# Thirteen tiles prepared in the opening of an attention layer, and the row maxima sent to the rows of q through memory

## What is computed

```python
xn = layernorm(x)
# attention: 16 heads of q, 8 of k and v (two q heads share one k and v), 16 wide
energy = einsum('nqhd,nkhd->nhqk', q, k) + alibi          # -|i-j| * 2**-(head+1)
attn = softmax(energy / sqrt(16))
att = einsum('nhqk,nkhd->nqhd', attn, v).reshape(n, s, 256) @ Wo.T + bo
# linear with quantised rows
x_scale = max(amax(abs(xn)), 1e-6) / 127
lin = (clip(round(xn / x_scale), -128, 127) @ weight_q.T) * x_scale * weight_scale + bias
out = x + att + lin
```

## Time and profile before

| | us |
|---|---|
| median of 3 runs | 1567.06 |
| the profiled execution, whole | 1568.38 |
| its span in the trace | 1566.4 |
| busy: TensorE / VectorE / ScalarE / GpSimd | 1497.0 / 1394.6 / 1184.8 / 1076.1 |

### The profile page before, as it was taken

The page is one execution under the profiler, slowest core; times in us unless marked ns, Lnnn a source line. Parts: engine busy times, 40 slices in busy tenths (PEclk is TensorE's granted clock), DMA queues, the critical chain, the costliest instruction groups (busy, mean ns, idle before and its releaser), DMA issues.

```text
span 1566.4 us, 42517 instructions
## 1 busy us (share of the span) xinstructions
PE 1497.0 (96%) x16284; PEld 583.0 (37%) x16284; DVE 1394.6 (89%) x1698; ACT 1184.8 (76%) x2331; POOL 1076.1 (69%) x1627
## 2 busy tenths in 40 slices
PE   5899999999999999999989999999999999999998
PEld 5333333333333333333333334333333333333333
DVE  5999989999899998999979999899998988999981
ACT  3467777777787776887767887777877777788885
POOL 5467777777788876787757877677877776533332
PEclk9999999999999999999999999999999999999999
DMA  6522243333334334333333433433333332312212
GB/s 169 140 76 71 74 100 81 93 98 81 105 83 108 96 79 109 91 92 101 84 92 94 105 85 91 103 98 96 97 83 96 94 92 65 82 49 68 72 44 62
DMA packets 197291, 140.98 MB, mean 90 GB/s; under 512 B 107040, under 2 KB 165728, under 8 KB 197088
## 3 DMA queue, kind: packets, MB, share of 16 engines
q1 hardware_dynamic: 197088, 138.27, 34.2%
HBM read 81.40 MB, written 35.63 MB: 75 GB/s over the span
## 4 chain that ended last, share of the span: by engine, by line
PE 47%; DVE 30%; SPq 9%; issue 8%; DMA 3%; POOL 2%; ACT 0%; POOLq 0%; DVEq 0%; ACTq 0%
DVE row_max L999 27%; PE ps_ring L1279 15%; PE ps_pv L1355 13%; PE ps_row L1296 9%; PE ps_ring L1395 4%; PE ps_ring L1415 3%; SPq L464 2%; SPq L468 2%; SPq L506 2%; DMA q<-neg_max_t 1%; SPq L472 1%; PE ps_ring L1398 1%; DMA k<-k_alibi 1%; DVE pv_turned L1039 1%; PE ps_ring L1409 1%
## 5 line engine op out<-in xcount | busy, mean ns | idle before, releaser
L999 DVE TENSOR_REDUCE row_max<-ps_row 128x1 f32<-128x1024 f32 x1024 | 1199.5, 1213 | 114.7 <-PE ps_row L1298 99.4
L1171 ACT ACTIVATE probs<-ps_ring 128x512 f32<-128x512 f32 x2048 | 1084.5, 601 | 245.2 <-PE ps_ring L1279 242.6
L1279 PE MATMUL ps_ring<-q,k 122*32 122x512 bf16 x8192 | 636.6, 383 | 19.9 <-DMA q<-neg_max_t 19.0
L762 POOL TENSOR_TENSOR probs<-probs,near 128x256 f32<-128x256 f32 x512 | 375.2, 733 | 324.8 <-ACT probs L1171 318.9
L1355 PE MATMUL ps_pv<-probs,v_unit 128*32 128x512 f32 x4096 | 533.5, 596 | 0.0
L1279 PEld LDWEIGHTS ps_ring<-q,k 122*32 122x32 bf16 x8192 | 215.1, 95 | 518.0 <-ACT probs L1171 324.7
L1296 PE MATMUL ps_row<-k,q 64*128 64x512 bf16 x944 | 326.2, 385 | 25.8 <-DVE row_max L999 11.4
L1298 PE MATMUL ps_row<-k_again,q_again 64*128 64x512 bf16 x944 | 326.0, 385 | 0.0
L1296 PEld LDWEIGHTS ps_row<-k,q 64*128 64x128 bf16 x944 | 84.2, 93 | 320.3 <-issue 199.6
L1355 PEld LDWEIGHTS ps_pv<-probs,v_unit 128*32 128x32 f32 x4096 | 124.7, 110 | 54.2 <-issue 7.7
L1298 PEld LDWEIGHTS ps_row<-k_again,q_again 64*128 64x128 bf16 x944 | 84.0, 92 | 0.0
(11 more groups left out here) (84 smaller groups left out, 1012.0 us busy)
## 6 DMA issues: line engine op xcount, KB each, us to landing
parts_dram<-parts SPq DMA_DIRECT2D x59, 288.0 KB, 3.0
q_again<-q SPq DMA_DIRECT2D x63, 256.0 KB, 3.3
token_b<-token_dram SPq DMA_DIRECT2D x53, 256.0 KB, 4.1
q<-parts_dram SPq DMA_DIRECT2D x128, 96.0 KB
k<-parts_dram SPq DMA_DIRECT2D x256, 32.0 KB
q<-parts_dram SPq DMA_DIRECT2D x128, 64.0 KB
att_dram<-att_unit SPq DMA_DIRECT2D x126, 64.0 KB
att_t<-att_dram SPq DMA_DIRECT2D x56, 128.0 KB, 2.9
```

Source lines behind the costliest of these rows:

```text
L762: pool.tensor_tensor(here, here, near[:, u % KV_HEADS, :].rearrange("p (e n) -> p e n", e=GROUP), ALU.mult).then_inc(weighted, 1)
L999: dve.tensor_reduce(row_max[:, par, e, qb:qb + 1], ps_row[qb % 2][:, :], AX_X, ALU.max, negate=True).then_inc(row_max_found, 1)
L1171: act.activation(probs[:, c % PBUFS, e, h * HALF:(h + 1) * HALF], ring_bank(u, c, e, h), ACT.Exp, scale=SCALE).then_inc(ring_freed, 1)
L1279: mm = pe.matmul(to[at, :], weights[:, at], moving, start=start, stop=stop)
```

## The change

Three things. **(1)** PREP_AHEAD goes from 11 to 13. The opening makes 13 tiles, tiles made in units come one pair earlier relative to their batch (tile 15 in unit 3), and late_set with all its branches goes: every set is loaded by next_set at the start of its unit, and every row block in the units is a half_row_block. In the opening the store of tile 8 goes ahead of the first set, the stores of the others behind set 1; the first rounding step of tiles 0 to 7 goes from GpSimd to VectorE (round_first), in place. In units 0 and 1 the normalising and statistics of the two tiles are spread over blocks 1 and 3. out_tile takes the place of near_bias. **(2)** place_max, four transfers inside SBUF, becomes store_max (neg_max_t to max_dram, one transfer) and place_max (max_dram to the two rows of q, one transfer, which waits for the store). **(3)** In SP's unit the order behind load_token is new: store_max(u+1), in even units store_att(u-1), load_again(u+3), place_max(u+1), load_att_t, store_out.

```diff
-PREP_AHEAD = 11
+PREP_AHEAD = 13
-OTHERS_BEHIND = [1 + 22 * k // 12 for k in range(PREP_AHEAD + 2)]
+OTHERS_BEHIND = [1 + 22 * k // (PREP_AHEAD + 1) for k in range(PREP_AHEAD + 2)]
-def late_set(u):
-
-    return u >= SETS - 1 and last_tile(u) >= PREP_AHEAD and made_unit(last_tile(u)) == u - SETS + 1
...
+            def store_max(u):
+
+                sp.wait_ge(max_turned, u + 1)
+                sp.dma_start(max_dram[u % PAIR, :, :].rearrange("x (j r) -> j x r", r=TURN),
+                             neg_max_t[:, :]).then_inc(max_stored, 16)
+
             def place_max(u, slot):
 
-                sp.wait_ge(max_turned, u + 1)
-                for j in range(P // TURN):
-                    sp.dma_start(q_set[SET_K:COL_K, slot, :, :].rearrange(
-                        "m e (a j r) -> m (e a) j r", j=P // TURN, r=TURN)[:, :, j, :],
-                        neg_max_t[j * TURN:(j + 1) * TURN, :]).then_inc(set_loaded[slot], 16)
+                sp.wait_ge(max_stored, 16 * (u + 1))
+                sp.dma_start(q_set[SET_K:COL_K, slot, :, :].rearrange("m e n -> m (e n)"),
+                             max_dram[u % PAIR, :, :].rearrange("(m x) n -> m (x n)", m=MAX_ROWS)).then_inc(
+                                 set_loaded[slot], 16)
...
-            for t in range(BLOCKS):
+            for t in range(BLOCKS + 1):
                 store_parts(t, t % 2)
-            wait_parts(BLOCKS, 0)
+            wait_parts(0)
             load_set(0, 0)
-            for t in range(BLOCKS, PREP_AHEAD):
-                store_parts(t, t % 2)
             sp.dma_start(near_bias[:, :, :], diag.rearrange("g p n -> p g n")).then_inc(
                 near_loaded, 16)
             load_set(1, 1)
+            for t in range(BLOCKS + 1, PREP_AHEAD):
+                store_parts(t, t % 2)
...
             store_token(PREP_AHEAD)
+            store_max(0)
+            load_again(2, 2)
             place_max(0, 0)
-            load_again(2, 2)
...
-                if u + 2 < UNITS and late_set(u + 2):
-                    load_again(u + 2, (u + 2) % SETS)
-                if f["row_set"] and not late_set(u + 3):
+                if f["row_set"]:
                     next_set(u + 3)
...
                 if not f["last"]:
-                    place_max(u + 1, (u + 1) % SETS)
+                    store_max(u + 1)
                 if f["prev"] and u % PAIR == 0:
                     store_att(u - 1)
+                if f["row_set"]:
+                    load_again(u + 3, (u + 3) % SETS)
+                if not f["last"]:
+                    place_max(u + 1, (u + 1) % SETS)
                 for t in f["next_att"]:
                     load_att_t(t, t % 2)
-                if f["row_set"]:
-                    if late_set(u + 3):
-                        next_set(u + 3)
-                    else:
-                        load_again(u + 3, (u + 3) % SETS)
...
+            def round_first(t):
+                dve.wait_ge(first_scale_ready, 2)
+                dve.wait_ge(xn_turned, t + 1)
+                dve.tensor_scalar(xn_of(t), xn_of(t), token_of(t)[:, XINV:XINV + 1], ROUND,
+                                  ALU.mult, ALU.add).then_inc(first_rounded, 1)
...
                 dve.wait_ge(max_split, 2 * (u + 1))
                 if u > 0:
-                    slot = (u - 1) % SETS
-                    dve.wait_ge(set_loaded[slot], set_count(u - 1, slot, WHOLE_SET))
+                    dve.wait_ge(max_stored, 16 * u)
...
-                        if not late_set(u + 2):
-                            wait_again(u + 2)
-                    if late_set(u + 2):
-                        row_block(u + 2, (u + 2) % SETS, 0, i - BLOCKS)
-                    else:
-                        half_row_block(u + 2, (u + 2) % SETS, 0, i - BLOCKS)
+                        wait_again(u + 2)
+                    half_row_block(u + 2, (u + 2) % SETS, 0, i - BLOCKS)
```

More of the change, by code:

```diff
@@ L125, in flags_of @@
         factor=[PREP_AHEAD + 2] * (u == 0) + [u + PREP_AHEAD + 3] * (u + PREP_AHEAD + 3 < TILES),
-        first_linear=([u // 2] if u < 18 else [9, 10] if u == 18 else []) if not pairs else [],
+        first_linear=([u // 2] if u < 18 else [9, 10] if u == 18 else
+                      list(range(11, PREP_AHEAD)) if u == 20 else []) if not pairs else [],
         xt=u + 2 + PREP_AHEAD < TILES,
@@ L157 @@
 SET_LOADS = K_LOADS + GROUP * Q_LOADS + ALIBI_LOADS
-WHOLE_SET = SET_LOADS + P // TURN
+WHOLE_SET = SET_LOADS + 1
 def alibi_rows():
@@ L190, in build @@
 def build(nc, x, x_t, wqk_t, wv_t, wo_t, wo_last_t, w8_t, w_scale, bias_attn, bias_lin, q_alibi, k_alibi, diag,
-          eye, parts_dram, token_dram, att_dram, out):
+          eye, parts_dram, token_dram, att_dram, max_dram, out):
     ctx = ExitStack()
@@ L256, in build @@
         att_last = sb("att_last", [P, EC, SEQ])
-        out_tile = sb("out_tile", [P, 2, EMBED])
+        out_tile = near_bias[:, :, :].rearrange("p g n -> p (g n)").bitcast(F32)[:, 0:2 * EMBED].rearrange(
+            "p (b n) -> p b n", n=EMBED)
         ps_row = [ctx.enter_context(nc.psum_tensor(f"ps_row{i}", [P, SEQ], F32)) for i in range(2)]
@@ L316, in build @@
         first_rows_loaded = sem("first_rows_loaded")
-        first_parts_stored = [sem(f"first_parts_stored{i}") for i in range(FIRST_PARTS)]
+        first_parts_stored = [sem(f"first_parts_stored{t}") for t in range(PREP_AHEAD)]
         first_amax_ready = sem("first_amax_ready")
         first_scale_ready = sem("first_scale_ready")
+        first_rounded = sem("first_rounded")
         first_lin_ready = sem("first_lin_ready")
@@ L356, in build @@
         max_turned = sem("max_turned")
+        max_stored = sem("max_stored")
         ring_filled = sem("ring_filled")
@@ L417, in wait_stored @@
         def wait_stored(eng, t):
+            if t < FIRST_PARTS:
+                return
             if t < PREP_AHEAD:
-                wait(eng, first_parts_stored[t % FIRST_PARTS], 16 * (t // FIRST_PARTS))
+                eng.wait_ge(first_parts_stored[t - FIRST_PARTS], 16)
             elif t < PREP_AHEAD + 2:
-                i = t % 2
-                eng.wait_ge(first_parts_stored[i], 16 * len(range(i, PREP_AHEAD, FIRST_PARTS)))
+                last = max(k for k in range(PREP_AHEAD) if k % FIRST_PARTS == t % 2)
+                eng.wait_ge(first_parts_stored[last], 16)
             else:
@@ L442, in store_parts, with wait_parts @@
                     parts_of(t).rearrange("p m (c n) -> p (m c) n", n=P)).then_inc(stored, 16)
[L444 to L448, removed]
+            def wait_parts(u):
+                last = last_tile(u)
+                for t in range(last + 1 - BLOCKS, min(last + 1, PREP_AHEAD)):
+                    sp.wait_ge(first_parts_stored[t], 16)
                 for t in (PREP_AHEAD, PREP_AHEAD + 1):
-                    wait(sp, parts_stored[t % 2], 16 * len(range(t, tiles, 2)))
+                    wait(sp, parts_stored[t % 2], 16 * len(range(t, last + 1, 2)))
             def load_set(u, slot):
@@ L709, in quantise @@
             def quantise(t):
[L711 to L715, removed]
+                if t >= BLOCKS:
+                    pool.wait_ge(first_scale_ready, 4)
+                    pool.wait_ge(xn_turned, t + 1)
+                    pool.tensor_scalar(xn_of(t), xn_of(t), token_of(t)[:, XINV:XINV + 1], ROUND,
+                                       ALU.mult, ALU.add).then_inc(first_rounded, 1)
+                pool.wait_ge(first_rounded, t + 1)
                 wait(pool, xq_turned, t - 1)
-                pool.tensor_scalar(xq[:, t % 2, :], xround[:, :], -ROUND, Q_MAX, ALU.add,
+                pool.tensor_scalar(xq[:, t % 2, :], xn_of(t), -ROUND, Q_MAX, ALU.add,
                                    ALU.min).then_inc(xq_ready, 1)
@@ L990, in _ @@
                     find_first_scales(0, BLOCKS, 0)
+                for k in range(max(0, PAIR * (t - BLOCKS + 1)), min(BLOCKS, PAIR * (t - BLOCKS + 2))):
+                    round_first(k)
             find_first_scales(BLOCKS, PREP_AHEAD, 2)
@@ L1069, in unit, with here @@
                 at_sums, at_norm = (5, BLOCKS) if apart else (3, 3)
+                made = 1 if u < PAIR else PAIR
+                def here(c):
+                    return slice(0, made) if c == 1 else slice(made, PAIR)
                 for c in range(BLOCKS):
@@ L1085, in unit @@
                             turn_back(u - 1)
-                    if c == 1:
-                        for t in f["normed"]:
+                    if c in (1, 3):
+                        for t in f["normed"][here(c)]:
                             normalise(t, t % 2)
@@ L1090, in unit @@
                             find_scale(t, t % 2)
-                        for t in f["stats"]:
+                        for t in f["stats"][here(c)]:
                             wait(dve, x_loaded, 16 * (t - X_AHEAD + 1))
@@ L1210, in _ @@
             for i in range(2, FIRST_PARTS):
```

(3 more changed lines are left out.)

10 lines of the change are left out of this document (6 added, 4 removed).

## The result

The changed kernel takes 1716.64 us in the median (1714.80 to 1718.91); the kernel before, run beside it, 1570.11. The ratio is 1.0932 (95% interval 1.0887 to 1.0976). 1709 was predicted. The profiled execution has a span of 1713.0 us, 146.6 more than before.

The account below looks back on a forecast made before the run. TensorE, busy 1497.0 of 1566.4 us, was taken to bound the kernel. 1566.4 + 111 + 37 + 22 - 27 - 3.9 + 3 = 1708.5 of span, so 1709 against 1567.06; range 1645 to 1759.

Parts of the forecast that it names:

- The main step: In 30 even units SP issues the load behind store_att and load_again, so the next unit starts 3.7 us late: +111.
- The bound "behind q_again": Upper bound for the load's landing in even units, queued behind q_again's 3.3 us: next unit 4.3 us late.
- the row of the 128 KB load: Profile row of a load from memory, 2.5 us issue to landing, taken as the time of the load of the maxima.
- The clock: Lower TensorE clock after 27 of the 30 waits, 1.39 us each: +37 (21 to 42).
- The odd units' waits: In 25 odd units store (3.5) plus load (2.5) land 0.9 us late for the next unit: +22 (0 to 47).
- Its 1672 for the sum: Total in us if each transfer leg took the skill page's 2.0 us; the odd units' wait would vanish.
- The gain: No late sets at the 7 batch boundaries, -27, and two tiles less among the units, -3.9.
- The opening: Unit 0 starts later through the store and load of its maxima and two more tiles: +3 (0 to 5).
- The first: Rival: load of the maxima not late in even units, no waits or slow clocks, 1539 us; chance 0.07.
- The second: Rival: even-unit waits come, but the clock stays up and odd units arrive in time, 1637 to 1650; chance 0.13.
- The third: Rival: store and load each take 4.5 us, even units 5.7 late, about 1799 us; chance 0.05.
- The fourth: Rival: wait and gain cancel, needing a delay of 1 us in 30 units; chance 0.01.

Follow-up runs that it names:

- experiment 3: Changed kernel with its 13 tiles in the opening, but the four transfers inside SBUF and SP's order of the kernel before; 1541.16 us, ratio 0.9826.
- experiment 7: Changed kernel with load_again issued behind the load of the maxima, store_att still ahead of it; 1626.47 us, ratio 1.0354.
- experiment 1: Changed kernel with store_att in even units issued behind the load of the maxima instead of ahead of it; 1561.62 us, ratio 0.9957.
- experiment 5: Changed kernel, SP's order untouched, with VectorE's turn of the output in even units after row block 9 instead of 13; 1565.22 us, ratio 0.9969.
- experiment 4: Kernel before (11 tiles, late sets) with the maxima by one store and one load, store_att behind the load; 1610.97 us, ratio 1.0271.
- experiment 8: Kernel of experiment 3 with the opening's 512 KB load of wo_last moved behind load_token; 1538.45 us, ratio 0.9796 to the kernel before.
- experiment 9: Changed kernel with SP's order store_max, place_max, store_att, load_again, the load of the maxima directly behind its store; 1547.65 us, ratio 0.9846.
- experiment 2: Kernel before with its four transfers inside SBUF moved behind store_att and load_again in SP's order; 1789.88 us, ratio 1.1411.
- experiment 6: Changed kernel with 48 useless matmuls run by TensorE in each odd unit from 3 on before it waits for the maxima; 1677.46 us, ratio 1.0681.

## Why the prediction was right, and where it was right by accident

**The main step held.** The waits stand where they were put (odd units 3 to 61), for the reason given (SP stands still for the turn), and the load goes out at 21.39 us of the unit where 21.4 was worked out. The term was 111 us; the waits are 114.8, and 5.4 more lie in the even units' busy time (20.05 against 19.86 in unit 12), which the sum didn't have; without the wait it isn't there (19.87 in experiment 3). The small error is in the load's leg: 2.9 in the median, not 2.5. The bound "behind q_again" was nearer than the row of the 128 KB load, and experiment 7 shows about 0.5 us of that neighbour. Experiments 1 and 5 remove the waits from two sides, by the order and by the turn.

**The clock was undersized.** 27 of 30 waits at 1.39 made 37. The lower clock came with all 30. The odd units took 54.3 longer; less the 3 us of the next paragraph that leaves some 51. In 24 units the stretch lasted about 3.4 us and cost 1.1 to 1.7 (median 1.48), 35 together. In six (15, 23, 29, 33, 43, 49) it lasted about 6.8 and cost 2.5 to 2.8 (unit 15: 28.54 against 26.00), 16 together. In these six the clock had fallen 0.6 to 1.2 us before TensorE started again; in the others it fell at most 0.5 us before the start, or up to 1.4 after it. Filling the idle time took 44.5 us from the odd units; so much is shown to be the clock's, and the rest rests on the comparison of unit lengths alone. The price for one stretch was nearly right (1.39 for 1.48); what failed is the count, 27 for 30, and that a stretch can last twice as long, which none of the three at such waits in the trace of before did.

**The odd units' waits were oversized.** 22 us were predicted, some 3 came: only five even units start over 0.3 us late for the load, the worst 0.83. The step that failed is the 2.5 for the load's second leg. The store took 3.3 in the median until the load's issue (3.5 predicted), but the load then took about 2.0 (1.6 to 2.5 in the 15 even units with any idle time at their start). With nothing of 256 KB just ahead of it (SP had stood still for 1.9 us behind q_again in unit 11) it was about as fast as the fastest of the earlier trace rows, 2.1. By the Trainium skill ("DMA: Bandwidth & Descriptors", "Anatomy of one DMA — SWDGE (gpsimd) path"), whose fixed cost of about 2.0 is fitted for the other issuing path, 2.0 for each leg (an estimate) would have removed these waits. The load agrees with that figure, the store at 3.3 doesn't, and in the last units, where little else moves, store to load is 1.9 too. Its 1672 for the sum fails on the even units, where the load took 2.9.

These two errors, 14 us too few and 19 too many, and the 9 too few of the even units leave 4; the nearness of 1709 to 1716.6 owes much to that, and is in so far luck. The 30 waits alone decide the sign.

**The gain held.** No late set is left, unit 14 is like 12, unit 51 is the last that makes tiles; -31.2 was measured where -30.9 stood. Experiment 3 has it by itself: its span is 26.9 below before, the 31.2 less what its opening costs.

**The opening.** +3.3 against +3. The working put part of it on the store and load of unit 0's maxima and part on the tiles. Either alone delays unit 0, from 68.72 to 71.57 by the trip (experiment 4) and to 74.20 by the tiles (experiment 3), and both together no more than the tiles alone (73.66). What holds SP up with 13 tiles is the opening's own queue, and one load moved out of the way starts unit 0 3.3 us earlier (experiment 8). But these are numbers of one trace each, and the opening varies: with the same opening as after, unit 0 starts at 78.60 in experiment 9, where SP comes to the maxima at 71.55 instead of 65.36. So the agreement of 3.3 with 3 shows little.

**Rivals.** The first (1539, load not late) describes what the same edit does in another order: 1547.65 in experiment 9. The second, a clock that stays up, is refuted by all 30 units. The third, 4.5 for each leg, by 2.9 and 2.0 for the load. The fourth, wait and gain cancelling, by 114.8 of waits against a gain of 31.2.

**What the expectations missed.** That of experiment 1 left out the copy of 256 KB just ahead of the load and load_again's wait for its set; that of experiment 2 was 5 us too low; that of experiment 4 allowed 1 to 2 us in each late unit for the trip and nothing for the clock behind it; and in experiment 9 the reason given for the gap was wrong (its rival had the gap right and the time wrong). What the store waits for in the middle units isn't settled: its gap goes with transfers issued just ahead of it, but whether it is the token, the set or the made tiles no run shows, since none took one of these away alone.

## What to carry to other kernels

On an in-order queue, ask of each instruction that is moved what the instruction ahead of it waits for; in experiment 9 the load could go out 3.8 us behind its store, and in after it went out 7.7 behind it, only because of what stood ahead of it. Replacing several small transfers by a store and a load saves issues, but adds a second landing, so it needs a place with cover for both (5.6 us in unit 11 of after, 7.2 in unit 14 of experiment 4), and whether that cover exists can depend on another part of the same change. Where a short wait of TensorE repeats, price the clock behind it as well, from several units that follow such a wait and not from one.

## What the runs showed of the hardware

- The lower clock came after idle times of 1.82 (experiment 6), 1.92 (experiment 5), 2.09 (experiment 7), 2.17 and 3.57 to 4.29 (after, 30 of 30), and didn't come after 2.13 (experiment 7), 2.98, and 2.23 and 2.51 (units 39 and 47 of before). In this range the length of the idle time alone doesn't tell it.
- Once down at such a wait, it stayed for about 3.4 us or, where it fell 0.6 us or more before TensorE started again, for about 6.8 us, in after (cost 1.1 to 1.7 and 2.5 to 2.8 us a unit).
- 48 matmuls without use in each of 30 idle times, with the units before them no shorter for it, made the kernel 39.2 us faster.
- A load of 8 KB from memory took about 2.0 us from issue to use (1.5 to 2.5), and 2.6 to 3.1 right behind a copy of 256 KB (after). The dependent store of 8 KB held its load back by 1.9 to 2.0 us where SP had issued nothing for 3.5 us ahead of it, and by 2.8 to 5.4 where its last issue was at most 1.5 us ahead (experiment 9).
- In the opening of after two issues of stores of 288 KB took 6.97 us of SP's time, 3.6 and 3.3 (0.6 for the one just before them): a transfer's issue can itself be held up, and what stands behind it with it.

```profile
43.70 6.97 SPq L441 DMA_DIRECT2D parts_dram<-probs  x2
```
